# Router logits in two groups of matmuls, negated router weights, masks beside the sum, and one low half on GpSimd

## The reference

```python
x = x + xattn(layernorm(x), ctx_2048)      # linear attention over 12544 context rows
x = x + attn(layernorm(x))                 # gated running sums, then a SwiGLU of width 2048
x = x + ffn(layernorm(x))                  # two experts of width 2048, top 1

def ffn(x, w_router, w_fc, w_proj):
    logits = x @ w_router.T                # 128 x 2
    probs = softmax(logits)
    top_idx = argmax(probs)                # the first where both are equal
    top_weight = probs[top_idx]
    h = einsum('nd,ehd->enh', x, w_fc)
    a = square(where(h >= 0, h, 0.5 * h))
    expert_out = einsum('enh,edh->end', a, w_proj)
    mask = (top_idx == arange(2)[:, None])
    return einsum('end,en->nd', expert_out, mask * top_weight)
```

## Time and profile before

| what | value |
|---|---|
| median of 3 runs | 862.51 us (862.4 to 862.77) |
| span of the profiled execution | 860.8 us |
| TensorE busy (matmul) | 851.4 us, 99% |
| VectorE busy | 683.3 us, 79% |
| ScalarE busy | 554.7 us, 64% |
| GpSimd busy | 370.6 us, 43% |

### The profile page before, as it was taken

One profiled execution on the slowest core, in us unless ns is written; L12 is line 12 of the kernel. 1 busy time (PEld: TensorE's weight loads), 2 busy tenths in 40 slices (PEclk: granted clock), 3 DMA queues, 4 the chain that ended last, 5 costly groups with the idle time before them and its releaser, 6 DMA issues.

```text
span 860.8 us, 14422 instructions
## 1 busy us (share of the span) xinstructions
PE 851.4 (99%) x4618; PEld 731.0 (85%) x4618; DVE 683.3 (79%) x1075; ACT 554.7 (64%) x1009; POOL 370.6 (43%) x215
## 2 busy tenths in 40 slices
PE   8999999999999999999999999999999999999998
PEld 7888888888888888888888888888888889878767
DVE  5777777777777777777777777888888878779897
ACT  5666666666666666666666666666777656676563
POOL 2555454544555554445445555544454433220000
DMA  7212214010101010010101010101101000679740
GB/s 271 98 51 76 73 52 167 24 49 24 49 24 49 24 49 25 30 43 24 49 24 49 24 49 24 48 25 28 46 24 49 26 1 11 239 282 410 308 147 13
DMA packets 19529, 66.25 MB, mean 77 GB/s; under 512 B 2224, under 2 KB 2992, under 8 KB 19120
## 3 DMA queue, kind: packets, MB, share of 16 engines
q1 hardware_dynamic: 19072, 64.88, 20.9%
q10 hardware_dynamic: 432, 1.05, 0.3%
HBM read 65.66 MB, written 0.26 MB: 77 GB/s over the span
## 4 chain that ended last, share of the span: by engine, by line
PE 91%; issue 4%; DVE 2%; DMA 1%; POOL 1%; ACT 0%; POOLq 0%; ACTq 0%; SPq 0%; DVEq 0%
PE kv_ps L879 11%; PE f_ps L866 11%; PE v_bank L784 10%; PE v_bank L785 10%; PE v_bank L786 10%; PE k_bank L784 10%; PE k_bank L785 10%; PE k_bank L786 10%; PE kv_ps L1178 2%; PE kv_ps L1160 1%; DMA early<-in_wk 1%; PE f_ps L949 0%; PE f_ps L1050 0%; PE v_bank L968 0%; DMA ctx_raw<-in_ctx 0%
## 5 line engine op out<-in xcount | busy, mean ns | idle before, releaser
L461 POOL TENSOR_TENSOR ksum_acc<-ksum_acc,kf 128x1024 f32<-128x1024 f32 x97 | 233.0, 2402 | 86.7 <-DVE kf L1284 86.7
L454 POOL TENSOR_TENSOR ctx_lo<-ctx_raw,ctx_hi 128x512 fp32r<-128x512 f32 x92 | 119.7, 1301 | 274.0 <-ACT ctx_hi L532 274.0
L540 ACT ACTIVATE keys<-k_bank,bias_cols 64x512 fp32r<-64x512 f32 (+1 forms) x194 | 131.5, 678 | 148.6 <-PE k_bank L786 146.2
L1260 DVE SCALAR_TENSOR_TENSOR keys<-k_bank,bias_cols,keys 64x512 fp32r<-64x512 f32 (+1 forms) x194 | 143.2, 738 | 83.7 <-ACT keys L540 80.4
L1277 DVE TENSOR_TENSOR kf<-f_ps,fb 128x256 f32<-128x256 f32 x392 | 148.6, 420 | 16.8 <-ACT fb L557 5.6
L784 PE MATMUL v_bank<-wv_hi,ctx_lo 128*128 128x512 f32 x388 | 152.3, 392 | 0.0
L785 PE MATMUL v_bank<-wv_lo,ctx_hi 128*128 128x512 f32 x388 | 152.1, 392 | 0.0
L784 PE MATMUL k_bank<-ctx_hi,wk_lo 128*128 128x512 f32 (+1 forms) x392 | 151.4, 386 | 0.0
L785 PE MATMUL k_bank<-ctx_lo,wk_hi 128*128 128x512 f32 (+1 forms) x392 | 151.1, 385 | 0.0
L786 PE MATMUL v_bank<-wv_hi,ctx_hi 128*128 128x512 f32 x388 | 151.0, 389 | 0.0
L786 PE MATMUL k_bank<-ctx_hi,wk_hi 128*128 128x512 f32 (+1 forms) x392 | 149.9, 383 | 0.0
(11 more groups left out here) (245 smaller groups left out, 979.0 us busy)
## 6 DMA issues: line engine op xcount, KB each, us to landing
ctx_raw<-in_ctx SPq DMA_DIRECT2D x46, 512.0 KB, 3.3
early<-in_stream SPq DMA_DIRECT2D x15, 1024.0 KB, 8.4
raw<-in_stream SPq DMA_DIRECT2D x12, 1024.0 KB, 8.7
early<-in_stream SPq DMA_DIRECT2D x8, 512.0 KB, 4.2
early<-in_ctx SPq DMA_DIRECT2D x2, 512.0 KB, 6.1
early<-in_wv SPq DMA_DIRECT2D x1, 1024.0 KB, 7.8
early<-in_wq SPq DMA_DIRECT2D x1, 1024.0 KB, 9.2
early<-in_wo SPq DMA_DIRECT2D x1, 1024.0 KB, 7.1
```

The source lines that it names most:

```text
L454: pool.tensor_tensor(ctx_lo[:, s, :, cols], raw[:, :, t % 2 * P:(t % 2 + 1) * P], ctx_hi[:, s, :, cols].bitcast(f32), ALU.subtract).then_i ...
L461: pool.tensor_tensor(ksum_acc[:, :].rearrange("p (j f) -> p j f", f=P), ksum_acc[:, :].rearrange("p (j f) -> p j f", f=P), kf[:, t % 2, :, ...
L540: act.activation(keys_2[rows, s, 2 * m + h, 0:n], src[rows, 0:n], ACT.Identity, bias=bias_cols[rows, KC + m:KC + m + 1]).then_inc(k_hi_rea ...
L1260: dve.scalar_tensor_tensor(out=keys_2[other, s, 2 * m + h, 0:n], in0=src[rows, 0:n], scalar=bias_cols[rows, KC + m:KC + m + 1], in1=keys_2 ...
```

## The change

It has four parts.

1. `logits(ks)` is called twice: for chunks 0 and 1 before `hi_hi` of chunks 2 and 3, and for chunks 2 and 3 behind that `hi_hi`, with the wait for act_lo moved ahead of it. `hi_lo` of chunks 2 and 3 comes behind the logits.
2. `wr_2` holds the negated router weights (ScalarE copies with scale -1, VectorE's low part is -w - high). So the logits in PSUM are negated, the minimum is the negated maximum, and the exponential is taken with scale -1 and that minimum as its bias. The step that negated the maximum is gone.
3. The steps behind the exponential are ordered anew, with explicit waits on the chain's counter: the comparison is issued behind the sum without waiting for it, the reciprocal waits for the sum, the complement for the comparison, the product for the complement, and one scaling by reciprocal and squared rstd comes last.
4. The low half of (GF_[2], 0) is left out of `PIECES`. GpSimd makes it, ahead of `rstd(3, 8, 1)` in its queue, once ScalarE's high half is there; TensorE waits for it on a semaphore of its own. VectorE makes no low piece between its statistics and the router, and the later stretches of `PIECES` are numbered one lower, with the same pieces.

```diff
-PIECES = [(g, h) for g in SPLIT for h in range(2)]
+POOL_PIECE = (GF_[2], 0)
+PIECES = [(g, h) for g in SPLIT for h in range(2) if (g, h) != POOL_PIECE]
...
+            low_half(pool, *POOL_PIECE).then_inc(pool_lo_ready, 1)
             rstd(3, 8, 1)
...
-            act.activation(wr_2[:, :, 0:2], w_router[:, :, :], ACT.Copy).then_inc(wr_hi_ready, 1)
+            act.activation(wr_2[:, :, 0:2], w_router[:, :, :], ACT.Copy, scale=-1.0).then_inc(wr_hi_ready, 1)
...
-            act.wait_ge(logit_neg_ready, 1)
-            act.activation(logit[:, 3:5], logit[:, 0:2], ACT.Exp, bias=logit[:, 2:3]).then_inc(expl_ready, 1)
+            act.wait_ge(logit_min_ready, 1)
+            act.activation(logit[:, 3:5], logit[:, 0:2], ACT.Exp, scale=-1.0, bias=logit[:, 2:3]).then_inc(expl_ready, 1)
...
+                elif (g, h) == POOL_PIECE:
+                    pe.wait_ge(pool_lo_ready, 1)
...
                 lo_hi(g, ps, act_lo, full, False, (0, 1))
+                if logits is not None:
+                    logits((0, 1))
                 pe.wait_ge(act_hi_ready, 2 * (n - 2) + 2)
                 hi_hi(g, ps, act_hi, full, (2, 3))
+                if logits is not None:
+                    pe.wait_ge(actT_ready, 2 * n)
+                    logits((2, 3)).then_inc(logit_done, 1)
                 hi_lo(g, ps, act_hi, full, (2, 3))
                 pe.wait_ge(actT_ready, 2 * n)
-                if logits is not None:
-                    logits()
                 lo_hi(g, ps, act_lo, full, True, (2, 3)).then_inc(group_used, 1)
...
-            dve.tensor_tensor(wr_2[:, :, 2:4], w_router[:, :, :], wr_2[:, :, 0:2].bitcast(f32), ALU.subtract)\
-               .then_inc(wr_ready, 1)
+            dve.scalar_tensor_tensor(out=wr_2[:, :, 2:4], in0=w_router[:, :, :], scalar=-1.0,
+                                     in1=wr_2[:, :, 0:2].bitcast(f32), op0=ALU.mult, op1=ALU.subtract).then_inc(wr_ready, 1)
...
-            low_pieces(26, 27)
-            dve.wait_ge(logit_done, 1)
+            def step(ins):
+                links[0] += 1
+                ins.then_inc(chain, 1)
+                return links[0]
+
             dve.wait_ge(rstd_ready, 3)
             dve.tensor_tensor(stat[:, 13:14], stat[:, 8:9], stat[:, 8:9], ALU.mult)
+            dve.wait_ge(logit_done, 1)
...
-            link(dve.tensor_reduce(logit[:, 2:3], logit[:, 0:2], AX.X, ALU.max))
-            dve.tensor_scalar(logit[:, 2:3], logit[:, 2:3], -1.0, None, ALU.mult).then_inc(logit_neg_ready, 1)
+            dve.tensor_reduce(logit[:, 2:3], logit[:, 0:2], AX.X, ALU.min).then_inc(logit_min_ready, 1)
             dve.wait_ge(expl_ready, 1)
-            link(dve.tensor_reduce(logit[:, 5:6], logit[:, 3:5], AX.X, ALU.add))
-            link(dve.reciprocal(logit[:, 5:6], logit[:, 5:6]))
-            link(dve.tensor_scalar(logit[:, 3:5], logit[:, 3:5], logit[:, 5:6], stat[:, 13:14], ALU.mult, ALU.mult))
-            link(dve.tensor_tensor(logit[:, 6:7], logit[:, 3:4], logit[:, 4:5], ALU.is_ge))
-            link(dve.tensor_scalar(logit[:, 7:8], logit[:, 6:7], -1.0, 1.0, ALU.mult, ALU.add))
-            link(dve.tensor_tensor(logit[:, 6:8], logit[:, 6:8], logit[:, 3:5], ALU.mult))
+            total = step(dve.tensor_reduce(logit[:, 5:6], logit[:, 3:5], AX.X, ALU.add))
+            first_wins = step(dve.tensor_tensor(logit[:, 6:7], logit[:, 3:4], logit[:, 4:5], ALU.is_ge))
+            dve.wait_ge(chain, total)
+            inverse_total = step(dve.reciprocal(logit[:, 5:6], logit[:, 5:6]))
+            dve.wait_ge(chain, first_wins)
+            second_wins = step(dve.tensor_scalar(logit[:, 7:8], logit[:, 6:7], -1.0, 1.0, ALU.mult, ALU.add))
+            dve.wait_ge(chain, second_wins)
+            winner = step(dve.tensor_tensor(logit[:, 6:8], logit[:, 6:8], logit[:, 3:5], ALU.mult))
+            dve.wait_ge(chain, max(inverse_total, winner))
+            link(dve.tensor_scalar(logit[:, 6:8], logit[:, 6:8], logit[:, 5:6], stat[:, 13:14], ALU.mult, ALU.mult))
```

## The result

| | before | after |
|---|---|---|
| median | 862.77 us (862.4 to 863.96, 21 runs) | 863.76 us (862.85 to 866.17, 21 runs) |
| span of the profiled execution | 860.8 us | 863.1 us |
| mean granted clock of the profiled execution | 1.000 | 0.998 |

The account below looks back on a forecast made before the run. TensorE, busy nearly the whole 860.8 us span, bounds the kernel, so only its stops count. Hold +2.2 and router -1.3 (cap 1.34, TensorE's removable wait for hid) make +0.9: 862.5 becomes 863.4 us, whole range 861.0 to 863.9.

Parts of the forecast that it names:

- The hold: Near 801.2 us GpSimd's low half blocks a two-input VectorE piece, delaying x1's transposes; 2.2 us lost.
- R1: Rival: VectorE is not held by GpSimd's low half, so only the router counts; -1.3, 861.2 us; chance 0.27.
- R2: Rival: GpSimd and VectorE take turns in parts, costing +0.6; with the router -0.7, 861.8 us; chance 0.17.
- R4: Rival: the rstd power stays long and VectorE is not held; -0.5, 862.0 us; chance 0.05.
- The earlier trace: GpSimd's x1 scaling, 770.59 to 772.69, left a VectorE low piece at an undisturbed 1.22 us; evidence against the full hold.
- (a): Router start: without the low piece beside it, GpSimd's rstd power takes 0.54 instead of 1.47 us; gain 0.93.
- R3: Rival: VectorE is held, but the power stays at 1.47 us, slow from idleness; +1.7, 864.2 us; chance 0.08.
- (b): Router logits: split into two groups, their last matmul ends at 809.19, just in time for the step at 809.21.
- (c): Negated router weights: one VectorE step in front of the exponential goes; gain 0.19 us.
- (d): Masks beside the sum behind the exponential: 0.97 to 1.05 us in place of 1.29; gain taken as 0.3.
- (e): The wr_2 step at 760.98 becomes a form with a multiply; cost 0 to 0.06 us, taken as 0.
- The router's sum of 1.3: The router's parts sum to 1.42 us; 1.3 gained at TensorE's wait for hid, nearly all of the 1.34 cap.

Follow-up runs that it names:

- a3: The whole change, but GpSimd waits until VectorE has made the 26 pieces in front of the residual sum before making its low half; 861.00 us, ratio 0.9976.
- b2: The whole change, but GpSimd makes only 512 of the 1024 columns and VectorE the other 512 behind the first hidden tile; 862.11 us, ratio 0.9993.
- d1: The whole change, but GpSimd makes both low halves of GF_[2] instead of one; 867.79 us, ratio 1.0059.
- a4: The whole change plus four unused fp32 matmuls on TensorE in front of the late x1 transposes, to fill its stop; 864.40 us, ratio 1.0014.
- d4: The whole change, but GpSimd copies the raw half (one SBUF input) instead of taking the difference, leaving out that subtraction; 861.78 us, ratio 0.9988.
- d3: The kernel before, with only VectorE's low piece moved from beside the power to behind the first hidden tile; 862.98 us, ratio 1.0003.
- b3: a3 with all eight logit matmuls again in one group behind hi_lo of chunks 2 and 3 (part 1 undone); 861.49 us, ratio 0.9987.
- a1: Parts 1 to 3 alone on the kernel before; the low half stays on VectorE, beside the power; 861.93 us, ratio 0.9986.
- a2: Part 4 alone, the low half on GpSimd, with the router of the kernel before; 864.63 us, ratio 1.0022.
- d2: a3 with the second block's low pieces moved and one more half, (GU[0], 1), made by GpSimd between its two rms powers; 860.92 us, ratio 0.9982.

## Why the prediction came out as it did

- **The hold, 2.2 us: right.** 2.21 more for the two pieces, 2.14 at the transposes, 2.2 from a3 against the kernel after, half with half the columns (b2), twice with two (d1). GpSimd won the first turn, as its 2.39 shows; in a4 it lost it, and the sum was the same. R1, R2 and R4 are refuted for this instruction. The earlier trace rows are not explained by that: the kernel after has the same scaling, and the pieces beside it again keep 1.22 each (two in 2.35 from 771.38). Why they are not held stays open: d4 shows that one input doesn't spare VectorE, and the scaling's two scalar operands were not tried.
- **(a) the power, 0.54 in place of 1.47: right.** 0.57 (after, a3, d3). That it was the piece beside it and not idleness is shown by d3, and R3 falls with it. (b) Logits just in time: right at full clock; in a3 rstd's squared step starts at 808.84, 0.04 behind the end of the power, and the first logit step at 808.96, right behind the last logit matmul (808.67 and 0.25), with no wait listed. In the profiled run of the kernel after, at the lower clock, that step did wait, 1.15. Against one group the split is worth 0.5 (b3).
- **(c) and (d), 0.5 together: right.** 0.6 in a1's span and 0.54 in its `hid` stop, and 0.96 from the sum to the first hidden tile, where 0.97 to 1.05 was said. (e) Nothing, as said.
- **The router's sum of 1.3: right, a little more.** The loads' stop went from 1.60 to 0.20; from the loads of the x1 transposes to those of `hid` it is 9.14 us before (805.03 to 814.17) and 7.71 in a3 (804.78 to 812.49), 1.43 less; a3's span is 1.5 under that of before. The cap of 1.34 was 0.1 short.
- **The sum: the term that it had at nothing.** At full clock 861.3 - 860.6 = +0.7 us of span (+2.2 - 1.5), where +0.9 was said, and only +0.5 of time, because the time outside the span, which "the change does not touch", is 0.2 us shorter; why is open. What lifts the median from there to +1.0 is the step that priced a stop of TensorE at its length: "The transposes go from 805.0 to 807.2 and everything behind moves along." In 10 of 21 runs the clock also fell, for 1.74 us more by the medians of the two groups; the one such run that was profiled worked 3.4 us at half the clock right behind the stop. So the near hit of +0.9 is partly two errors that cancel. d1's windows show the same level at its stop, and its time the price. That the stop raises the chance rests on counts: 14 of 32 runs with a stop of 2.3 us (the kernel after and a2) and all 5 with 4.4, against 24 of 198 runs of the kernels without it, among them 0 of 11 where the stop was filled (a4). Those 24, 13 of them of the kernel before, have no profile, and where their falls lie isn't known; some of the 14 may be of their kind.
- **What the number means: the step that failed.** "A measurement here can tell about 0.2% from no change, 1.7 us": the two groups of 21 runs told 0.06% to either side, 0.5 us. By that bound a forecast of +0.9 us was put at 0.87 for no change; with 0.5 us in its place the same cases (0.43 for the forecast, 0.08 for R3) give "slower" about a half and "faster" under a half, and the likeliest case would have been called slower. No run shows the bound of 0.2%; the three runs at hand lay within 0.37 us of each other.

## What to carry to other kernels

A GpSimd operation put beside a row of VectorE differences that read two SBUF tiles is not free because GpSimd has nothing else to do: it costs the row nearly its whole length (2.2 of 2.39 us), and a short GpSimd step on the critical path is stretched in the same way when such a VectorE piece stands beside it (the power, 0.57 us, to 1.47). Move the work all the same, but hold it with one wait until VectorE's critical row is done (a3: one line, from 863.76 to 861.00 us, against 862.77 before). The stops of TensorE of 2.3 and 4.4 us had a second price behind them, so put such a stop into the sum as its length plus a chance of some microseconds at half clock, and take the smallest difference that counts from the scatter of the runs, not from a round per cent.

## What was not expected of the hardware

- With a stop of 2.3 us of loads (1.9 of matmuls) the mean granted clock was below 1 in 14 of 32 runs; the one of them that was profiled had 3.4 us at 0.50, from 1.5 us behind the end of the stop. With a stop of 4.4 us it was below 1 in 5 of 5; the profiled one had 0.50 from about 807.4, within the stop, to 814.2 us.
- GpSimd and VectorE changed turns at the end of each instruction even where the other's next one stood ready: 5.67 us for two differences on GpSimd and 6.71 for two on VectorE, side by side (d1), where alone they took 2.4 and 1.2 each.
- A GpSimd copy with one input, 1.05 us long, held a two-input VectorE difference for 0.84 us, while the scaling of the earlier trace rows did not.
- The time outside the span was 1.83 us in the kernel after and in a3, 2.03 in the kernel before and 2.2 in d2, though none of these edits touches the start or the end of the program.
